# The keys' spread transfers issued by GpSimd, and a new list of steps, in a sixteen-batch transformer kernel

## The reference

```
h = layernorm(x) * (1 + ca) + sa
x = x + ga * attn1(h)          # 16 heads of 8 channels, causal over 512 tokens
h = layernorm(x) * (1 + cb) + sb
x = x + gb * ffn(h)            # 2 layers, each:
    #   qkv = shift(h) @ wqkv; q, k = rotary(l2norm(q)), rotary(l2norm(k))
    #   h += attention(q, k, v), windows of 64 with look-back, 8 heads of 64 channels, @ wo
    #   h += (a * gelu(g)) @ w2,  a, g = split(layernorm(shift(h)) @ w1)
# attn1: q = h @ W_UQ; k = (h @ W_DKV) @ W_UK; v likewise; softmax(q k / sqrt(8)) v @ W_O
```

## Time and profile before

| | |
|---|---|
| median of three runs | 2433.9 us (2421.71 to 2438.56) |
| the profiled execution | 2427.62 us, span 2425.8 us |
| PE busy in the span | 2183.1 us (90%) |
| DVE, ACT, POOL busy | 1646.6, 1587.9, 563.6 us |
| PE waits for batch 0's spread transfers | 25.3 us, once |
| a pair of batches repeats every | 289.8 us |
| granted TensorE clock, mean | 0.979 |

### The profile page before, as it was taken

One profiled execution on the slowest core, in us unless ns is written; L12 is line 12 of the kernel. 1 busy time (PEld: TensorE's weight loads), 2 busy tenths in 40 slices (PEclk: granted clock), 3 DMA queues, 4 the chain that ended last, 5 costly groups with the idle time before them and its releaser, 6 DMA issues. The chain is left out here.

```text
span 2425.8 us, 52449 instructions
## 1 busy us (share of the span) xinstructions
PE 2183.1 (90%) x21002; PEld 1383.2 (57%) x21002; DVE 1646.6 (68%) x2617; ACT 1587.9 (65%) x3047; POOL 563.6 (23%) x528
## 2 busy tenths in 40 slices
PE   3599899998999899998999989999899989999897
PEld 2455656556565466655565555655656546666454
DVE  2465877676866768667776676776776676866664
ACT  1267766767667676676666776667766767667664
POOL 2012330222302412024210243012330231202410
PEclk9799999999999999999999999999999999999998
DMA  3300132001320012100220012300131001320001
GB/s 100 61 9 17 32 58 43 2 17 37 58 39 17 14 35 54 31 17 16 51 55 12 17 32 46 50 6 17 37 53 43 17 1 37 52 36 18 16 17 25
DMA packets 62521, 78.67 MB, mean 32 GB/s; under 512 B 9266, under 2 KB 57004, under 8 KB 59948
## 3 DMA queue, kind: packets, MB, share of 16 engines
q1 hardware_dynamic: 62284, 75.33, 16.0%
HBM read 11.40 MB, written 4.19 MB: 6 GB/s over the span
## 5 line engine op out<-in xcount | busy, mean ns | idle before, releaser
L872 DVE TENSOR_REDUCE nm<-ps 128x2 f32<-128x768 f32 (+3 forms) x384 | 388.4, 1042 | 121.6 <-PE ps L562 114.8
L1009 POOL TENSOR_TENSOR pr<-pr 128x1024 f32<-128x1024 f32 x128 | 302.2, 2361 | 678.9 <-DVE pr L910 678.9
L805 ACT ACTIVATE pr<-ps,wb,inv 128x128 f32<-128x128 f32 x1024 | 370.6, 490 | 97.8 <-DVE wb L927 97.8
L505 PE MATMUL ps<-cf,pr 128*128 128x128 f32 x2048 | 284.6, 279 | 100.4 <-POOL pr L1019 69.0
L505 PEld LDWEIGHTS ps<-cf,pr 128*128 128x128 f32 x2048 | 225.7, 141 | 161.9 <-POOL pr L1019 81.7
L762 ACT ACTIVATE pr<-ps 128x896 f32<-128x896 f32 x256 | 233.4, 921 | 70.3 <-PE ps L580 67.0
L903 DVE TENSOR_TENSOR pr<-ps,rot 128x1024 f32<-128x1024 f32 x128 | 156.5, 1223 | 149.2 <-ACT pr L777 143.7
L777 ACT ACTIVATE pr<-ps 128x1024 f32<-128x1024 f32 x128 | 131.1, 1025 | 143.8 <-PE ps L628 81.4
L580 PE MATMUL ps<-Q,K 128*128 128x512 bf16 (+3 forms) x1024 | 223.7, 299 | 0.0
L561 PE MATMUL ps<-K,Q 128*128 128x128 bf16 x1024 | 196.6, 222 | 28.2 <-DMA K<-Kf 25.3
L921 DVE TENSOR_REDUCE wm<-ps 128x8 f32<-128x1024 f32 x128 | 156.7, 1224 | 69.0 <-PE ps L659 68.0
(11 more groups left out here) (151 smaller groups left out, 4453.3 us busy)
## 6 DMA issues: line engine op xcount, KB each, us to landing
pr<-V SPq DMA_DIRECT2D x32, 520.0 KB, 4.7
Q<-Kf SPq DMA_DIRECT2D x224, 64.0 KB
K<-Kf SPq DMA_DIRECT2D x224, 64.0 KB
pr<-V SPq DMA_DIRECT2D x32, 390.0 KB, 6.2
xn<-in_L_attn_x SPq DMA_DIRECT2D x16, 256.0 KB, 2.8
out<-hT SPq DMA_DIRECT2D x16, 256.0 KB, 2.2
Q<-in_c_edge SPq DMA_DIRECT2D x32, 64.0 KB
Q<-mT SPq DMA_DIRECT2D x128, 4.0 KB
```

Source lines behind the costliest of these rows:

```text
L505: mm = pe.transpose(dst[:, t * P:(t + 1) * P], src(t), ident)
L805: ins = act.activation(P2[s][:, 2 * (p % 2) + r, o:o + P], bank[:, r * T + o:r * T + o + P], ACT.Exp, scale=inv[s][:, t, h:h + 1], bias=wb ...
L872: dve.tensor_reduce(nm[s][:, qt, h0:h0 + n], src, AX_X, ALU.max, negate=True).then_inc(nm_r[s], 1)
L1009: pool.tensor_tensor(t1[s][t % 3], t1[s][t % 3], t2[s], ALU.add).then_inc(sum_r[s], 1)
```

## The change

Three things change, and no arithmetic does.

1. The keys' 14 spread transfers of a batch are issued by POOL, in the `proj` step, behind its own splitting of q and k. SP keeps the queries' 14. The new semaphore `spread_k` counts them, and PE waits for it too before `max 0`.
2. A table `PLACES` puts the groups of a stream's list in another order (for example `values` and `load` earlier or later among the others); before, the order was that of `steps()`. The same table serves both streams.
3. The string of bits `ALL` and the digits `FIRST_BANKS` are new.

```diff
-SPREADS = 16 * 2 * (2 * SLOTS + 1)
+SPREADS = 16 * 2 * (SLOTS + 1)
...
+PLACES = [
+    0, 1, 4, 3, 2, 5, 6, 7, 8, 9, 15, 10, 11, 16, 12, 17, 18, 19, 20, 13, 21, 23, 22, 14, 24, 25, 26, 27, 28, 31,
...
-    rest = [iter([[(s + S2 * (k - back), name) for back, name in names[i:j]] for k in range(B // S2 + 1)
-                  for i, j in zip(firsts, firsts[1:])]) for s in range(S2)]
+    groups = [names[i:j] for i, j in zip(firsts, firsts[1:])]
+    rest = [iter([[(s + S2 * (k - back), name) for back, name in groups[i]] for k in range(B // S2 + 1) for i in PLACES])
+            for s in range(S2)]
...
+        spread_k = Sem(sems("spread_k"), 16 * 2 * SLOTS)
...
                         if u == 0:
                             pe.wait_ge(*spread_r.at(b, SPREADS))
+                            pe.wait_ge(*spread_k.at(b, 16 * 2 * SLOTS))
...
+                        for part, done in enumerate((hi_r, mid_r, lo_r)):
+                            pool.wait_ge(*done.at(b, 2))
+                            for slot in [k for k in range(SLOTS) if K_PART[k] == part]:
+                                for r in range(2):
+                                    dst = K1[s][64 * r + D1 * slot:64 * r + D1 * (slot + 1), r * R1:(r + 1) * R1, :]
+                                    pool.dma_start(dst, parts[s][3 + part][64 * r:64 * r + 64, :]).then_inc(spread_k[s], 16)
...
-                        for i, slots in enumerate((Q_PART, K_PART)):
-                            for part, done in enumerate((hi_r, mid_r, lo_r)):
-                                sp.wait_ge(*done.at(b, i + 1))
-                                for slot in [k for k in range(SLOTS) if slots[k] == part]:
-                                    for r in range(2):
-                                        rows = slice(64 * r + D1 * slot, 64 * r + D1 * (slot + 1))
-                                        dst = Q1[s][rows, :, :] if i == 0 else K1[s][rows, r * R1:(r + 1) * R1, :]
-                                        sp.dma_start(dst, parts[s][3 * i + part][64 * r:64 * r + 64, :]).then_inc(spread_r[s], 16)
+                        for part, done in enumerate((hi_r, mid_r, lo_r)):
+                            sp.wait_ge(*done.at(b, 1))
+                            for slot in [k for k in range(SLOTS) if Q_PART[k] == part]:
+                                for r in range(2):
+                                    dst = Q1[s][64 * r + D1 * slot:64 * r + D1 * (slot + 1), :, :]
+                                    sp.dma_start(dst, parts[s][part][64 * r:64 * r + 64, :]).then_inc(spread_r[s], 16)
```

More of the change, by code:

```diff
@@ L88, in steps @@
     return between + [(0, name) for name in out[:cut]]
[L94 to L99, removed]
+PLACES = [
[5 rows of a table added]
+]
+ALL = ("1028000158306a00748393aedb76ffeb5271dc805294abd48abddab4920c8a6b6562befaa5144c005650e5abb6ddbffab49c772024a5"
+       "2af3429ef6ab2483229af4589fbda94515001594393aedb76ffead471dc890494adcd09bbdaaa920c8c675962eef6a5144c005650e56"
+       "bb6ddbffad51c772024a52af542aef6aca4832293f4549fbdc94515001594393aedb76ffead471dc809294ced50abbdab2920c8a67d1"
+       "64befa651454005650e56bb6ddbffab51c772220a52b73229ef6aaa4832296f454afbec945130026a8396aedb76ffead271dc809294a"
+       "bcd09bbdab2920c8a4f6954bef6a51454004e50e5abb6ddbffab51c7722112533b9426ef6aca4824a6f3a8568b9616697fed49421021"
+       "6e9dd345bdbf5bada5d1c0b212256d7c66ffffffc")
 def merged():
@@ L111, in merged @@
             out += [(b, name) for b, name in group if 0 <= b < B]
-    assert len(out) == B * len(names)
+    assert len(out) == B * len(names) and sorted(PLACES) == list(range(len(groups)))
     return out
 ORDER = merged()
[L119 to L144, removed]
@@ new lines @@
+FIRST_BANKS = ("010101230426023062400245240604526002467642046026402062706024602146026270467024602460410610420640274206762046"
+       "204620402606742602410243026036701620456206426745407647623012310241051041041014013021030243270627670674562764"
+       "570623454504523645012014615423052463257032637016701670237623012301601201201672676017054726107240160120624301"
+       "240132632450324530162402146201240620124206526045674024602460230123062342562046203640263026432064206420410210"
+       "460240634602326042604260406202346206410647062072301260452602462343503243267016701640150140140104107160170647"
+       "630263230234526324530236454203254654012015614523042563245032435014501450253245014501201401401234232013076342"
+       "103240625404206104561045245670456740215604162401460240146402742607236046204620450145024564724062405260425042"
+       "654206402460410610420640274206762046204620402606742602410243026036701620456206426745407652475601502310231021"
+       "021012014051040542630243230236724326730245676706745245016014215467054623547067546017601760546754015401601501"
+       "401674670162312740231401620140246501460154254670546750214604162401460240146402742067236046204620450145024564"
+       "724062405260425042654206402460410610420640274206762046204620402606742602410243026036701620456206426745407647"
+       "623012301240150140140104103210230243270627670674562764570623454504523623014012613245032465327067326017601760"
+       "326732013201601301201672676017054724105420643202460542305234654012501452601420542601640260164602562405234064"
+       "206420670167026746526042607240627062476204602640610410620460256204542064206420602404562402610263024034501420"
+       "674204624565705465423012301260170160160106103126736230416021040546752456740423676706723423016012413267032645"
+       "327067326017601760326732013201601320210672676107145725014520643202406106721067467230623760142063204610621461"
+       "062604364203452062406240670167046726346024607420647064276402604620610210640260436402324062406240604202364204"
+       "610465042052301240672402642363703264763201204510410510140104103120130234650425450456742546750452676405476276"
+       "014017216745064723546076547016701670547654015401601501401674676017023746107640265404620764507456276014701674"
+       "021640764201260420126204724067456026402640167016420102420642061420647460276042604260210610240620472406764026"
+       "402640204606724604210425046056701640236406246723207627645014501420130120120102105140150425470647670672364762"
+       "370645232302345645012014615423052463527067326017601760326732013201601301201672676017054724105204605424062102"
+       "341023623450234520613402146201240620124206526405674024602460230123062342562046203640263026432604206240210410"
+       "260420652604546024602460206404526406210627064074501460234604264523205436235401546017601701061016015046756451"
+       "206102430236724326730245676706745245016014215467054623547067546017601760601761071061061041067067456235427326"
+       "634236234504567236723673232323672367")
```

## The result

The changed kernel takes 2452.0 us (median of 10 runs, 2441.53 to 2457.81), the kernel before in the same rounds 2430.73: a ratio of **1.0083**, 95% interval 1.0062 to 1.0103. The forecast was a gain of 25 us; it is a loss of 21. The time lies inside the stated range (2385 to 2465), on the wrong side of the kernel before.

A forecast was written before the change was run, and what follows sets the result against it. PE, busy 90% of the span, bounds the kernel. A period's gains and new stall sum to -2.1 us, seven hand-overs to -14.7, with the start -25: 2433.9 to 2409 us, range 2385 to 2465.

The forecast's parts named there:

- The issues end at 8.7 + 14d = +17.8, K has landed at +20.3: Even batches, us after `proj` starts on PE: POOL's 14 issues at d = 0.65 us each, then 2.5 us lag.
- a clock that stays up longer: PE's products behind the even-batch `heads` stall: half of what the slow 1.2 GHz products cost, credited as -0.8 us a period.
- rival of shared engines: Spread transfers: POOL's and SP's queues share the engines that move data, so the kernel gets slower; chance 0.15.
- Sharing in full: All POOL transfers use SP's half of the DMA engines: K lands at +29.7, +75 us, about 2505 us.
- half case: Half of POOL's transfers use SP's half of the DMA engines: K and Q land at +23.9, +10 us, 2443.
- that half is the pattern of one queue: Argument against shared DMA engines: the 53% busy share reflects how one queue picks engines, about 8 of 16.
- The price of an issue: Time one `dma_start` holds POOL, called d: taken as 0.65 us, as on SP, bounded by 0.3 and 1.4.
- POOL held too long: Even batches' `proj`: fourteen issues delay POOL's addition and scaling; at 1.2 us an issue 2476 us; chance 0.20.
- The start: Batch 0's `max 0`: with K's transfers issued by POOL, PE starts at 71.5 and not 81.85, -10.3 us.
- The new list: Reordered steps shorten PE's waits at `turn` (1.6 us) and `pturn` (0.8), against +0.5 elsewhere: -1.9 us a period.
- -2.1 a period: Even-batch hand-over: credit for PE's old 2.09 us wait for POOL at `heads`, whose place the new stall takes.
- the list gives nothing back: Stalls won at `turn` and `pturn` reappear at the next wait; only the gain at batch 0 remains, 2424 us; chance 0.15.

The follow-up runs named there:

- e3: Changed kernel, with SP issuing Q's transfers only after all of K's have landed, to measure rates; 2563.1 us in its one run.
- e2: Kernel before, old list and banks, with only K's 14 transfers moved to POOL; 2462.6 us, ratio 1.0145 to the kernel before.
- e5: Changed kernel with `max 0` of even batches from 2 on moved to just before `max 1`; 2420.8 us, ratio 0.9968 to the kernel before.
- e1: Changed kernel's new list and banks, with all 28 spread transfers issued by SP again; 2478.4 us, ratio 1.0207 to the kernel before.
- e8: Changed kernel with late even `max 0`, K issued by POOL in odd batches and SP in even ones; 2404.2 us, ratio 0.9897 to the kernel before.
- e6: Changed kernel with late even `max 0`; in even batches POOL issues K in `values`, behind the first k scaling; 2424.1 us, ratio 0.9976 to the kernel before.
- e4: Changed kernel with 7 of K's 14 transfers left out, arithmetic instructions all kept; 2398.7 us, ratio 0.9875 to the kernel before.

## Why the prediction was wrong

**The step that failed** is "The issues end at 8.7 + 14d = +17.8, K has landed at +20.3". Its first half held (+16.7, in batch 8 +18.4), its second didn't: K was there at +24.2 to +27.7, because its transfers were priced with the lag of an undisturbed transfer. With Q out of the way that price is right: by +20 in e3. To land by +20.3 they would have had to move some 100 GB/s (0.92 MB in 9.1 us) beside Q's 79, 180 in all; the two move 106. The forecast had a shortfall of 2.3 us for K and of 2.7 for the scaled k, and so a stall of 2.7; K's alone became 6.9. To this comes time at the lower clock: by the mean granted clock, 0.979 before and 0.965 after, 4.2% and 7.0% of the span passed at 1.2 GHz, 102 and 172 us. The forecast had credited 0.8 us a period for a clock that stays up longer. That K at +25 or later would show it wrong was among its own signs.

**It was the rival of shared engines**, to which I gave 0.15, in a form between its two cases. Sharing in full put K at +29.7, the half case at +23.9, and measured is +26.9 in the mean; over SP's queue alone the rate grew by a third, not by nothing and not to double. The half case's 2443 is near the measured 2452, in part by luck: it has the landing 3 us too early and leaves out the time at the lower clock. (Full sharing, +75, makes 2509, not 2505.) The argument that I used against it ("that half is the pattern of one queue") took a busy share of 53% for 47% that another queue could have. The busy share is the time packets take, and packets of two queues take longer side by side (e3).

The Trainium skill, "DMA: Bandwidth & Descriptors", "Issuing engines are not separate DMA queues", says that transfers started by different engines run on the same 16 DMA engines, and that several issuers save only the time of issuing. I cited that page twice and not this section. The traces agree in that the two rates don't add up: 106 GB/s together where 200 would be the sum. They show more than that too: together the two are slower than POOL's queue alone (123) and faster than SP's (77).

**The price of an issue** was taken somewhat too high: 0.56 us against 0.65, so fourteen hold POOL for 7.9 us and not 9.1. Only in batch 8, with the pause, is it 9.5.

**POOL held too long (0.20)** is not what decided, but the mechanism is there: e2's 6 to 8 us at `heads`, e5's 3.6 to 5.3. My path for it (second addition, scaling of k, transposes) costs 1.2 us in batches 2, 4 and 12, less than the 2.7 it was priced at. In 6, 8, 10 and 14 a longer one, through DVE and ACT, ends later (e5).

**The start** was put at -10.3 us and came out at +1.4. Batch 0's `max 0` begins at 76.67, not at 71.5, and waits 22.0 us instead of 25.3 (with the old list, 20.8): both queues move there too. And the new list asks for batch 1's `max 0` when Q has not landed: 9.0 us of wait, where PE stood 1.4 before.

**The new list.** Its -1.9 a period were `turn` (-1.6) and `pturn` (-0.8) against 0.5. `turn` came as counted (12.4 us over eight periods, 1.6 each), `pturn` went the wrong way (+1.8), and nmb, which was not counted, gave 1.2. The scaled k's -18.8 us are for the most part the stall for which -2.1 a period was already credited. With that term, -4.0 were forecast and the waits named here fell by 3.3 (26 us). The rival that the list gives nothing back (0.15) is right for `turn` and `pturn`, 12.4 won and 14.1 lost, and not for the whole: in e1 the waits on K grew by 73 us and the time only by 49.

With K at +26.9 in the forecast's own sum, a period becomes -2.1 + (8.9 - 2.7) = +4.1; measured, +4.5. That is close in part by luck: PE came to `max 0` 1 us later than the forecast's +18.0, `pturn` and the clock cost more than it had them, and nmb gave what it had not counted. How much each is worth, no run separates.

## What to carry to other kernels

A second issuing queue takes over the issuing, not the moving: before counting on it, put the bytes of both queues against what each moves while it runs alone, and don't add the two rates (here 106 GB/s together for 77 and 123 apart). No run here lets POOL issue both Q and K, or has K moved ahead of Q in a schedule meant to be fast. Price a transfer's landing from rows with the same neighbours, and when a schedule pulls its consumer forward, ask whether bytes over rate still fits; where it doesn't, move the consumer (e5: -31 us). When a wait ends with A, look up what was waiting 1 us behind it, and give each issuer the batches in which nobody waits for that engine (e8).

## What the runs showed of the hardware

- POOL and SP send the same transfer in different packets: 10752 for 224 transfers of POOL are 48 each; SP's 224 make up 62284 - 46156 = 16128, or 72 each, by part 3 of the pages of before and after. Alone, POOL's queue moves 123 GB/s at a busy share of 49% while it issues without a break, SP's 77 at 56% (e3).
- Beside each other both slow down: the same packets take 118 us of 16 engines instead of 56 (POOL's queue) and 305 instead of 277 (all of SP's), at 106 GB/s and a busy share of 90%. What they share (engines, ports, or memory) no run here tells apart.
- POOL issues a 64 KB transfer of this shape in 0.56 us, SP in 0.61.
- In each of the five kernels in which POOL issues 224 transfers (after, e2, e3, e5, e6) it pauses once, for 1.64 to 2.00 us, between the 113th issue and the 114th: the first two of batch 8. The profile puts the pause to the issuing itself. The two kernels with 112 issues (e4, e8) have none. Whoever reads batch 8 alone takes it for a cost of every batch.
